# One semaphore per recurrent step, attention in 32-column tiles, and zero products in the prologue of a four-layer kernel

## The reference, cut to what matters

```python
def step(carry, xz_t):
    prev_h, prev_c = carry
    z = xz_t + prev_h @ Wh
    ai, af, ao, ag = jnp.split(z, 4, axis=1)
    i = jax.nn.sigmoid(ai)
    f = jax.nn.sigmoid(af)
    o = jax.nn.sigmoid(ao)
    g = jnp.tanh(ag)
    next_c = f * prev_c + i * g
    next_h = o * jnp.tanh(next_c)
    return ((next_h, next_c), next_h)
...
x = x + _L0_cond_ref(...)
x = x + _L1_cond_ref(...)
x = x + _L2_cond_ref(...)
x = x + _L3_cond_ref(...)
```

## Time and profile before

| | before |
|---|---|
| median of 3 runs | 1958.13 us (1957.75 to 1960.11) |
| the profiled execution's own time | 1957.56 us |
| its span, first to last instruction | 1955.8 us |
| TensorE products / weight loads, busy | 97% / 74% of the span |
| VectorE / GpSimd / ScalarE busy | 71% / 58% / 42% |
| chain that ended last: TensorE / ScalarE / VectorE | 87% / 6% / 4% |
| mean granted TensorE clock | 0.996 |

### The profile page before, as it was taken

How to read it: one execution, slowest core, us unless ns; L and a number is a source line. 1 busy time by engine, 2 the same in 40 slices (tenths; PEclk the granted TensorE clock), 3 DMA queues, 4 the chain that set the end, 5 groups by cost and what they waited for, 6 DMA issues and landing times.

```text
span 1955.8 us, 256304 instructions
## 1 busy us (share of the span) xinstructions
PE 1889.5 (97%) x113680; PEld 1439.8 (74%) x113680; DVE 1390.7 (71%) x7217; ACT 827.2 (42%) x4757; POOL 1133.8 (58%) x4950
## 2 busy tenths in 40 slices
PE   7999999999999999999999999999999999999998
PEld 5777777777777777777777777777777777777776
DVE  2677777777777777777777777777777777777776
ACT  1344444444444444444444444444444444444444
POOL 4555655655555565565555556555555655665565
PEclk9899999999999999999999999999999999999999
DMA  4000000000000000000000000000000000000000
GB/s 170 4 4 3 3 4 3 3 3 4 3 3 4 3 3 3 4 3 3 4 3 3 4 3 3 3 4 3 3 4 3 3 3 4 3 3 4 3 3 3
DMA packets 57724, 14.67 MB, mean 8 GB/s; under 512 B 56176, under 2 KB 56304, under 8 KB 57200
## 3 DMA queue, kind: packets, MB, share of 16 engines
q1 hardware_dynamic: 57712, 14.50, 3.2%
HBM read 12.37 MB, written 2.10 MB: 7 GB/s over the span
## 4 chain that ended last, share of the span: by engine, by line
PE 87%; ACT 6%; DVE 4%; issue 2%; DMA 0%; POOL 0%; DVEq 0%; SPq 0%; POOLq 0%; ACTq 0%
PE psum L953 29%; PE psum L943 29%; PE psum L815 10%; PE psum L836 7%; PE psum L855 6%; DVE h_ring L703 3%; ACT o_act L532 3%; ACT psum L535 2%; PE psum L798 2%; PE psum L829 2%; PE psum L843 1%; PE psum L892 1%; PE psum L793 0%; DMA wkv_sb<-in_wkv 0%; PE psum L776 0%
## 5 line engine op out<-in xcount | busy, mean ns | idle before, releaser
L943 PEld LDWEIGHTS psum<-wh_sb,h_ring 128*2 128x2 f32 (+1 forms) x32768 | 488.4, 90 | 416.6 <-DVE h_ring L703 409.8
L953 PE MATMUL psum<-h_ring,wh_sb 128*32 128x2 f32 x65536 | 765.7, 173 | 1.8 <-issue 1.8
L953 PEld LDWEIGHTS psum<-h_ring,wh_sb 128*32 128x32 f32 x65536 | 725.8, 109 | 2.0 <-issue 2.0
L943 PE MATMUL psum<-wh_sb,h_ring 128*2 128x64 f32 (+1 forms) x32768 | 656.8, 220 | 50.8 <-DVE h_ring L703 20.2
L526 ACT ACTIVATE f_act<-psum 128x4 f32<-128x4 f32 x1024 | 177.3, 173 | 698.6 <-DVE psum L744 698.6
L744 DVE STREAM_TRANSPOSE psum<-psum 128x64 f32<-128x64 f32 x1024 | 266.1, 260 | 274.6 <-PE psum L943 262.7
L815 PE MATMUL psum<-up_sb,x 128*32 128x256 f32 (+1 forms) x3096 | 311.8, 460 | 0.0
L746 DVE STREAM_TRANSPOSE psum<-psum 128x64 f32<-128x64 f32 x1024 | 271.5, 265 | 1.9 <-PE psum L943 1.9
L703 DVE SCALAR_TENSOR_TENSOR h_ring<-o_act,psum 128x4 f32<-128x4 f32 x1025 | 163.0, 159 | 141.9 <-ACT psum L535 115.9
L836 PE MATMUL psum<-down_e,hid_t 128*16 128x256 f32 x3096 | 251.6, 382 | 0.6 <-ACT down_e L507 0.6
L756 DVE TENSOR_TENSOR_SCAN psum<-addend,psum 128x16 f32<-128x16 f32 x1024 | 199.3, 195 | 52.2 <-ACT psum L529 2.4
(11 more groups left out here) (142 smaller groups left out, 2286.0 us busy)
## 6 DMA issues: line engine op xcount, KB each, us to landing
x_a<-in_x SPq DMA_DIRECT2D x129, 16.0 KB, 1.6
x_s<-in_x SPq DMA_DIRECT2D x129, 16.0 KB, 1.6
up_sb<-in_up SPq DMA_DIRECT2D x1, 2048.0 KB, 12.7
out_y<-y_sb SPq DMA_DIRECT2D x128, 16.0 KB, 1.4
down_sb<-in_down SPq DMA_DIRECT2D x1, 1536.0 KB, 8.3
wx_sb<-in_wx SPq DMA_DIRECT2D x1, 1024.0 KB, 14.5
wh_sb<-in_wh SPq DMA_DIRECT2D x1, 1024.0 KB, 16.6
wkv_sb<-in_wkv SPq DMA_DIRECT2D x1, 512.0 KB, 4.4
```

Source lines behind the costliest of these rows:

```text
L943: last = nc.tensor.matmul(z[32 * j:32 * j + row + B, :], h_ring[:, prev, c, WIN - B - row:WIN], wh_v[:, c, g, j, :], start=False, stop=(c ...
L953: last = nc.tensor.matmul(by_row(z)[32 * j:32 * (j + 1), m, row:row + B], wh_v[:, c, g, j, 32 * m:32 * (m + 1)], h_ring[:, prev, c, WIN - ...
```

## The change

It has four parts. `hid` becomes eight semaphores, one for each step; `close` increments the next step's by 8, and TensorE makes one register for a whole loop turn, `t + U`, in place of seven. GpSimd waits on `hid[0]` where it waited on `hid`. `attend` writes its 256 columns in eight tiles of 32 in place of four of 64. VectorE first sets a tile `idle_w` to zero, and TensorE multiplies it by itself: twice with 512 columns before it waits for the first weights, once with 512 after L776, and once with 256 after the first scores. The results, in bank 4, are not read.

```diff
+        idle_w = sb("idle_w", [P, 512])
...
-        hid = sem("hid")
+
+        hid = [sem(f"hid_{u}") for u in range(U)]
...
-            for s in (f_made, i_made, o_made, f_turned, a_f, cell, cell_tanh, hid, x_turned, i_based):
+            for s in (f_made, i_made, o_made, f_turned, a_f, cell, cell_tanh, x_turned, i_based, *hid):
...
-                pool.wait_ge(hid, i * U + (READY + U + 1))
+                pool.wait_ge(hid[0], i * U + (READY + 2 * U))
...
+            nc.vector.memset(idle_w[:, :], 0.0).then_inc(idle_set, 1)
...
-                                               op0=ALU.add, op1=ALU.mult).then_inc(hid, 1)
+                                               op0=ALU.add, op1=ALU.mult).then_inc(hid[(slot + 1) % U], U)
...
+            def idle_mm(n):
+
+                nc.tensor.matmul(bank[4][:, 0:n], idle_w[:, 0:P], idle_w[:, 0:n], start=True, stop=True)
+
+            pe.wait_ge(idle_set, 1)
+            idle_mm(512)
+            idle_mm(512)
             pe.wait_ge(bank_clear, 2)
...
             last.then_inc(kv_made, 1)
+            idle_mm(512)
             pe.wait_ge(w_in["wq"], 16)
...
-                    for j in range(0, P, 64):
-                        last = nc.tensor.matmul(attn[j:j + 64, c], value_w[:, c * P + j:c * P + j + 64], weights,
+                    for j in range(J):
+                        last = nc.tensor.matmul(attn[32 * j:32 * (j + 1), c],
+                                                value_w[:, c * P + 32 * j:c * P + 32 * (j + 1)], weights,
...
             last.then_inc(first_scores, 1)
+            idle_mm(256)
             pe.wait_ge(value_out, 2)
...
+
+                now = pe.snap(t + U)
                 for u in range(U):
                     prev = (u - 1) % U
-                    now = pe.snap(t + (u + 1))
-
-                    pe.wait_ge(hid, now)
+
+                    pe.wait_ge(hid[u], now)
```

More of the change, by code:

```diff
@@ L225, in cond_stack_kernel @@
         cleared = sem("cleared")
+        idle_set = sem("idle_set")
         bank_clear = sem("bank_clear")
```

## The result

| | before | changed |
|---|---|---|
| median | 1958.28 us (4 runs) | 2006.22 us (4 runs) |
| ratio | | 1.0238, 95% interval 1.0218 to 1.0258 |
| the profiled execution's own time / span | 1957.56 / 1955.8 us | 2004.81 / 2003.0 us |
| loop turn near 1000 us | 14.85 us | 15.23 us |
| first loop step starts | 42.13 us | 41.41 us |

The change costs 47.9 us where 20 were forecast as gained. (One of its four executions took 2145.94 us, at a granted clock of 0.75; the ratio leaves it out, and no trace of it exists.)

The account below looks back on a forecast made before the run. The prediction took the loop's ring of engines handing on h to bound the kernel, with one step held longer by the attention. 1957.6 − 15.2 (attention) − 5.0 (zero products) + 0.6 (median) gave 1938 us, range 1932 to 1946.

Parts of the forecast that it names:

- One register and eight semaphores: nothing: Loop steps: one register for seven and eight semaphores raised by 8 for one change no time; 0 us taken.
- The part on the register instructions: TensorE's loop: 896 register instructions of 32 ns, done while it waits for h; up to 8 us gain, none taken.
- The attention: Loop step with the attention: 32-column tiles no longer wait, saving 0.12 us in each of 127 turns, 15.2 us.
- a price for each product: Attention in the loop: each product costs 0.031 us whatever its width; +32 us, 1985 us, chance 0.05.
- only half of the idle time going: Attention in the loop: draining is not the cause, or half goes; gain 0 to 8 us, 1945 to 1953, chance 0.10.
- The zero products: Prologue: dense zero products raise TensorE from the 1.2 to the 2.4 GHz level earlier; 5.0 us gained.
- the first rival of the prediction: Prologue: the zero products do not hold the clock up; 1944 us, chance 0.22.
- The first turn: First loop turn, 44 to 66 us, granted clock 0.69: the dip may change, −6 to +3 us, 0 taken.

Follow-up runs that it names:

- the one raised by 1: The changed kernel with each of its eight semaphores raised by 1, and a second TensorE register that counts turns: 1944.17 us, ratio 0.9934.
- the run with 2: The kernel before with its one semaphore raised by 2, and one register instruction more on TensorE in each step: 2012.50 us, ratio 1.0281.

## Why the prediction was wrong

**The step that failed** is "One register and eight semaphores: nothing", and in it the sentence "VectorE's increment by 8 costs what one by 1 does". It costs 0.061 us in each of 1024 steps, 62 us (changed kernel against the one raised by 1). It rested on no row, and rows of the same trace spoke against it: the waits ahead of increments by 8 on L591, L399 and L482 stood apart. I had asked what of TensorE's waits was hidden and never what an increment does to the instruction that carries it, although that instruction is the one link of the ring that the change edits in every step. There was a hint to weigh: the Trainium skill, page "Trainium Kernel Development and Optimization", section "Key Constraints", says that compute semaphores must be raised by 1. This case does not bear out the must (the kernel raises others by 8 and works, and so does the run with 2), and the page gives no price; the runs do.

**The part on the register instructions** was right on time and wrong on worth. Their removal gains no time by itself, as far as the reverse shows (with eight idle instructions more than before: 1958.42 us). But it keeps the loop body at 1791 instructions. With them the 32-column attention would not gain 15 us, it costs 550. My table of rivals held nothing of the code's length, though the first turn's idle gaps, which I named "the code's first pass", and the 9 instruction packets were on the page. The Trainium skill, page "TensorE: Matmul & The Clock Gate", section "Step-by-step: what each phase is for", speaks of a 64-byte MATMUL instruction. A packet carries 5.75 MB / 351, 16.4 KB, so by that figure, as an estimate, 256 instructions, and seven packets 1792. That fits the runs: a body of just 1792 is not loaded again and one of 1798 is. It stays an estimate, since no run tried 1793 to 1797 and a turn that loads again takes nine packets, not seven or eight.

**The attention** was right, point by point: loads 0.07 us behind L849, products about 0.01 us apart (16 in 0.33 us), h the last to come, a turn of 14.74 us. 15.2 us were forecast, 13.9 measured. The rivals against it (a price for each product, or only half of the idle time going) are out. That emptying the array is what held the 64-column tiles back was argued from the rows; the runs show only that tiles of 32 columns do not wait.

**The zero products**: 5.0 us forecast, 0 measured. The level of L787 came as expected and was gone at 8.1 us. This is the first rival of the prediction, which had 0.22 and 1944 us, and 1944.17 is what the kernel raised by 1 takes. So without the increment's 62 us the forecast of 1938 would have missed by 6 us, most of it in this term. Why the level fell is not shown: the narrow products behind are the likely reason, since the trace of before had such products not raising it, but the run made to fill them with dense ones did not reach the level in its profiled execution.

**The first turn** keeps its dip (0.50 from 50 to 62 us), as taken.

The parts add up to the turn: 14.85 − 0.11 for the attention + 8 × 0.061 = 15.23 us. Over 128 turns that is +48.6 us, and with 0.7 less up to the first loop step 47.9, what was measured. That the last figure is met so closely is partly luck: the 0.061 comes from the same medians, and the 0.7 is no more than executions differ by.

## What to carry to other kernels

On a ring of engines that hand one value on, raise the semaphore by 1 in the instruction that also waits, and if the waits are to share one register, let that one count turns. Where a trace of the kernel before is at hand, look in it for an instruction that already does what the change will make others do; here it had hundreds. Before adding instructions to a long unrolled loop, look at the instruction packets on the page: a count that grows with the turns means that the body no longer fits, and then each instruction removed may be worth more than the time it takes. Test the parts of such a change one by one; here the increments cost 53 us alone, and the attention costs 550 alone but gains 14 once the register instructions are gone.

## What the runs showed of the hardware that was not expected

- An increment of 2 or 8 on a VectorE instruction that also waits makes the wait an instruction of its own (896 of 21 ns), and the write of h starts 0.10 us behind its releaser instead of some 0.04: 0.06 us a step. ScalarE and GpSimd have such separate waits of 17 ns ahead of their increments by 8; what they cost was not measured.
- TensorE's loop body of 1798 to 1806 instructions was loaded again in some of the loop's turns (6 to 46 of 128), nine packets of 16.4 KB each time, at 15 to 18 us a turn, with stalls of up to 5.2 us at the branch and mean granted clocks of 0.96 to 0.82 over the execution. At 1792 instructions and below: 9 packets in all and, in the profiled executions, a clock of 0.99 or more.
- After two dense products of zeros, 3.6 to 3.8 us long, TensorE ran at 2.4 GHz in three profiled executions and at 1.2 in a fourth. In the changed kernel's the clock fell again at 8.1 us, after 0.65 us without work and 1.8 us of narrow products.
